# Statistics of x: from inside the pair loop to a loop of their own, in the causal-mean stage of a slot-routing block

## The chip, the cores and the metric

One Trainium2 chip, 8 cores. Each core runs the same program on its own batch element: x of 4096 x 1024 float32, all weights whole. The time is in device microseconds of the slowest core, from a run of the whole program. There is no communication between cores.

## The reference

```
# per core: x is [4096, 1024]
def ln(v): return (v - mean(v)) / sqrt(var(v) + 1e-5)       # over the 1024 columns

u   = ln(x)
m_t = mean of u[0..t]            # causal softmax of zeros: a running mean over rows
x2  = x + ln(m)
y   = ffn(ln(x2))                # routing with top 8 of 64 slots, slot update (GRU),
                                 # slot attention, layer norm, two 1024x1024 products,
                                 # and the slots spread back over the 4096 rows
out = x2 + ln(y)
```

Only the part up to x2 is touched by the change.

## The kernel before, in words

x stays in SBUF as `sb_x`, 32 tiles of 128 rows by 1024 columns, loaded by eight DMAs of four tiles each on the SP queue (`semX[0..7]`, L252). Everything up to the first matmul of the stage also waits for the weights `sb_w1b` and a short initial product.

The program is written by hand, engine by engine; each engine executes its instructions in the order in which they are written, and semaphores tie the engines together. `Guard.emit` counts VectorE's instructions in `sSVG` and ScalarE's in `sSSG`, so that a wait for `V(("cC", pr), 0)` is a wait for one named instruction.

The causal-mean stage works in pairs of tiles (`NPAIR` = 16) and groups of four tiles (`NG` = 8):

- VectorE, per group: eight half-tile `bn_stats` of x into `bn6x`, eight small instructions (`combine`) that make a mean and a variance per row (`cA`), a wait for ScalarE's square root (`sq1`), and three small instructions (`post`, `pA`) that make scale and bias.
- ScalarE, per tile: `x1b` = scale * x + bias in bfloat16 (four buffers).
- TensorE, per tile j: the triangular matrix times x1b(j), plus, for odd j, the matrix of ones times x1b(j-1), plus the carry row, into `pcs[j % 3]`; and the column totals of the pair into `ptot`. Once per pair ScalarE copies `ptot` to the one-row `carry` (`cv`), which the next pair needs.
- VectorE, per pair: four `bn_stats` of `pcs` into `bn6c`, `combine` (`cC`), a wait for `sq2`, and `post` (`pC`).
- ScalarE, per tile: `anb` = the normalised running mean, from `pcs`; POOL adds it to `sb_x` (L432).

VectorE's program today is one loop over groups: the statistics of a group of x, then two pairs of the running mean. ScalarE's loop over tiles runs, at each even tile, first `sq2` of the pair before, then the carry copy, then (at every fourth tile) `sq1` of the group, then `x1b` of this tile and `anb` of the tile two before. POOL also issues seven weight casts (float32 to bfloat16 in HBM, L290 to L296) once all loads of x have landed.

After the stage come: routing (L475 to L600), slot input, the slot update with streamed weights, and the output stage.

Of the kernel before, what the change touches and what calls it, by code (L numbers as in the profile page):

```python
# [9 lines left out]
AF = mybir.ActivationFunctionType  # L10
# [16 lines left out]
NT = 32  # L27
D = 1024
DH = 512
# [50 lines left out]
def _build(stage, prev=None):  # L80
    V = (prev or {}).get
# [35 lines left out]
    with es:  # L117
# [6 lines left out]
        c_e2 = sbt("s_e2", [P, NT])  # L124
        c_one = sbt("s_one", [P, P], BF16)
        stat = sbt("stat", [P, 16 * NT])
        SM_MX, SM_VX, SM_G1, SM_S1, SM_B1 = 0, 1, 2, 3, 4
        SM_MC, SM_VC, SM_G2, SM_S2, SM_B2 = 5, 6, 7, 8, 9
# [31 lines left out]
        sCS = sem("sCS"); sBS = sem("sBS"); sX2 = sem("sX2")  # L160
# [3 lines left out]
        sSVG = sem("sSVG"); sSSG = sem("sSSG")  # L164
# [3 lines left out]
        val = {}  # L168
# [3 lines left out]
        def VTT(out, a, b_, op):  # L172
            return gv.emit([out], [a, b_], lambda: v_.tensor_tensor(out, a, b_, op=op))  # L173

        def VTS(out, a, s1, s2, op0, op1=None):
            ins = [a] + [x for x in (s1, s2) if x is not None and not isinstance(x, float)]
            if op1 is None:
                return gv.emit([out], ins, lambda: v_.tensor_scalar(out, a, s1, None, op0=op0))  # L178
            return gv.emit([out], ins, lambda: v_.tensor_scalar(out, a, s1, s2, op0=op0, op1=op1))

        def VSTT(out, a, scl, b_, op0, op1, accum=None):
            ins = [a, b_] + ([scl] if not isinstance(scl, float) else [])
            outs = [out] + ([accum] if accum is not None else [])
            return gv.emit(outs, ins, lambda: v_.scalar_tensor_tensor(  # L184
                out, a, scl, b_, op0=op0, op1=op1, accum_out=accum))

        def VRED(out, a, op, absv=None):
            return gv.emit([out], [a], lambda: v_.tensor_reduce(
                out, a, axis=AX, op=op, apply_absolute_value=absv))

        def VBN(out, a):
            return gv.emit([out], [a], lambda: v_.bn_stats(out, a))  # L192
# [4 lines left out]
        def VRC(out, a):  # L197
            return gv.emit([out], [a], lambda: v_.reciprocal(out, a))
# [4 lines left out]
        def SACT(out, in_, func, bias=0.0, scale=1.0, accum=None):  # L203
            extra = [x for x in (bias, scale) if not isinstance(x, float)]
            outs = [out] + ([accum] if accum is not None else [])
            return gs.emit(outs, [in_] + extra,
                           lambda: s_.activation(out, in_, func, bias=bias, scale=scale,  # L207
                                                 accum_out=accum))

        def SC(k, j, n=1):  # L210
            return stat[:, k * NT + j:k * NT + j + n]

        def combine(km, kv, bn6, pj, n, extra_e2):
            view = bn6[:].rearrange("p (j g k) -> p j g k", k=3, g=4)[:, pj:pj + n]
            mus = view[:, :, :, 1]
            cvs = view[:, :, :, 2]
            t0 = tmp4[:, 0:4 * n].rearrange("p (j g) -> p j g", g=4)
            a2 = tmp4[:, 16:16 + n]
            b1_ = tmp4[:, 20:20 + n]
            b2_ = tmp4[:, 24:24 + n]  # L220
            b3_ = tmp4[:, 28:28 + n]
            c1_ = tmp4[:, 32:32 + n]
            VRED(SC(km, pj, n), mus, OP.add)
            VTT(t0, mus, mus, OP.mult)
            VRED(a2, cvs, OP.add)
            VRED(b1_, t0, OP.add)
            VTT(b2_, SC(km, pj, n), SC(km, pj, n), OP.mult)
            if extra_e2 is None:
                VTS(b3_, a2, 1.0 / 1024.0, EPS, OP.mult, OP.add)
            else:  # L230
                VSTT(b3_, a2, 1.0 / 1024.0, extra_e2, OP.mult, OP.add)
            VSTT(c1_, b1_, 0.25, b3_, OP.mult, OP.add)
            return VSTT(SC(kv, pj, n), b2_, -1.0 / 16.0, c1_, OP.mult, OP.add)

        def post(ks, kb, kg, km, pj, n, sco=40):
            VRC(SC(ks, pj, n), SC(kg, pj, n))
            VTS(tmp4[:, sco:sco + n], SC(km, pj, n), -0.25, None, OP.mult)
            return VTT(SC(kb, pj, n), tmp4[:, sco:sco + n], SC(ks, pj, n), OP.mult)

        NG = NT // 4  # L240
        NPAIR = NT // 2
# [14 lines left out]
        def _(g):  # L256
# [17 lines left out]
        bn6c = sb1("bn6c", [P, NT * 12])  # L274
        pcs = [es1.enter_context(nc.psum_tensor("pcs0", [P, D], F32)),
               es1.enter_context(nc.psum_tensor("pcs1", [P, D], F32))]
# [57 lines left out]
        @blk.vector  # L334
        def _(v):
            v.wait_ge(semC, 64)
            for g in range(NG):
                v.wait_ge(semX[g], 16)
                for j in range(4 * g, 4 * g + 4):
                    VBN(bn6x[:, j * 12:j * 12 + 6], sb_x[:, j * D:j * D + DH])  # L340
                    VBN(bn6x[:, j * 12 + 6:j * 12 + 12], sb_x[:, j * D + DH:(j + 1) * D])
                val["cA", g] = combine(SM_MX, SM_VX, bn6x, 4 * g, 4, None)
                v.wait_ge(sSSG, V(("sq1", g), 0))
                val["pA", g] = post(SM_S1, SM_B1, SM_G1, SM_MX, 4 * g, 4)
                for pr in (2 * g, 2 * g + 1):
                    if pr >= 1:
                        v.wait_ge(sSSG, V(("sq2", pr - 1), 0))
                        val["pC", pr - 1] = post(SM_S2, SM_B2, SM_G2, SM_MC, 2 * (pr - 1), 2, sco=44)
                    v.wait_ge(sCS, 2 * pr + 2)
                    for j in (2 * pr, 2 * pr + 1):  # L350
                        VBN(bn6c[:, j * 12:j * 12 + 6], pcs[j % 3][:, 0:DH])
                        val["bn6c", pr] = VBN(bn6c[:, j * 12 + 6:j * 12 + 12], pcs[j % 3][:, DH:D])
                    val["cC", pr] = combine(SM_MC, SM_VC, bn6c, 2 * pr, 2, c_e2[:, 2 * pr:2 * pr + 2])
            v.wait_ge(sSSG, V(("sq2", NPAIR - 1), 0))
            val["pC", NPAIR - 1] = post(SM_S2, SM_B2, SM_G2, SM_MC, 2 * (NPAIR - 1), 2, sco=44)

        @blk.scalar
        def _(sc):
            sc.preload_act_table(AF.Sqrt)
            sc.wait_ge(sINI, 2)  # L360
            pass
            for j in range(NT + 3):
                if j >= 2 and j % 2 == 0 and (j - 2) // 2 < NPAIR:
                    pr = (j - 2) // 2
                    sc.wait_ge(sSVG, V(("cC", pr), 0))
                    val["sq2", pr] = SACT(SC(SM_G2, 2 * pr, 2), SC(SM_VC, 2 * pr, 2), AF.Sqrt)
                if j >= 1 and j % 2 == 0 and (j // 2 - 1) < NT // 2:
                    sb_i = j // 2 - 1
                    sc.wait_ge(sBS, sb_i + 1)
                    val["cv", sb_i] = SACT(carry[:], ptot[0:1, :], AF.Identity)  # L370
                if j % 4 == 0 and j < NT:
                    g = j // 4
                    sc.wait_ge(sSVG, V(("cA", g), 0))
                    val["sq1", g] = SACT(SC(SM_G1, 4 * g, 4), SC(SM_VX, 4 * g, 4), AF.Sqrt)
                if j < NT:
                    sc.wait_ge(sSVG, V(("pA", j // 4), 0))
                    if j >= 4:
                        sc.wait_ge(sCS, j - 3)
                        sc.wait_ge(sBS, (j - 2) // 2)
                    val["x1", j] = SACT(x1b[:, (j % 4) * D:(j % 4 + 1) * D],  # L380
                                        sb_x[:, j * D:(j + 1) * D], AF.Identity,
                                        bias=SC(SM_B1, j), scale=SC(SM_S1, j))
                if j >= 2 and (j - 2) < NT:
                    jj = j - 2
                    sc.wait_ge(sSVG, V(("pC", jj // 2), 0))
                    if jj >= 3:
                        sc.wait_ge(sX2, jj - 2)
                    val["an", jj] = SACT(anb[:, (jj % 3) * D:(jj % 3 + 1) * D],
                                         pcs[jj % 3][:], AF.Identity,
                                         bias=SC(SM_B2, jj), scale=SC(SM_S2, jj))  # L390
# [839 lines left out]
```

## Time and profile before

| | us |
|---|---|
| median of 4 runs | 872.04 (870.32 to 876.44) |
| profiled execution | 872.29 |
| its span, slowest core (5) | 870.7 |
| causal-mean stage on core 5, from the first bn6x to the last bn6c | 71.75 to 313.07 |

The profile is of the slowest core. The chain of waits starts at the end and follows each step back to what released it; its rows give start, duration, engine, what is written, the line, and how many instructions are merged. `bn6x` is the statistics of x (also used again in later stages), `bn6c` those of the running mean.

### The profile page before, as it was taken

How to read it: one execution, taken by the hardware profiler on the slowest of the kernel's cores; microseconds unless marked ns; L12 is line 12 of the kernel's file. 1: busy time of each engine (PE TensorE's matmuls, PEld its weight loads, DVE VectorE, ACT ScalarE, POOL GpSimd, SP SyncE). 2: the span in 40 equal slices, each digit the busy share in tenths (PEclk: the TensorE clock that was granted, in tenths of full speed). 3: DMA queues.
4: the chain of work that ended last, by engine and by line, in shares of the span. 5: the costliest groups of instructions: out<-in, count | busy, mean ns of one | idle time of the engine just before them, and what ended most of it. 6: DMA issues, size and time to landing. Idle time of an engine off the chain costs nothing.

```text
span 870.7 us, 7011 instructions; the slowest of 8 cores (861.9 to 870.7 us)
## 1 busy us (share of the span) xinstructions
PE 358.1 (41%) x1737; PEld 129.3 (15%) x1737; DVE 342.9 (39%) x1049; ACT 275.8 (32%) x344; POOL 163.2 (19%) x91
## 2 busy tenths in 40 slices
PE   0002363454436336688683246631123565222220
PEld 0001000000000003334342222211111111000000
DVE  0004535443452556564511015550020202888883
ACT  0001343434234254655833017720001101233332
POOL 2001242233324240000000010000000000665564
PEclk9999555555555555879985555555555555555555
DMA  7996989999890001000003540025513132224224
GB/s 202 250 281 173 121 97 122 108 108 118 100 121 0 0 8 30 1 1 2 1 1 73 108 74 0 2 60 121 114 32 108 45 87 62 96 97 176 113 99 191
DMA packets 69287, 76.29 MB, mean 88 GB/s; under 512 B 53216, under 2 KB 57312, under 8 KB 68640
## 3 DMA queue, kind: packets, MB, share of 16 engines
q0 software_dynamic: 4800, 22.25, 22.6%
q1 hardware_dynamic: 64448, 53.60, 20.9%
q8 instruction: 15, 0.25, 0.1%
q14 instruction: 24, 0.20, 0.1%
HBM read 68.72 MB, written 36.70 MB: 121 GB/s over the span
## 4 chain that ended last, share of the span: by engine, by line
PE 30%; DVE 30%; DMA 13%; issue 8%; ACT 8%; another core or an unknown queue 8%; DVEq 1%; POOLq 0%; ACTq 0%; POOL 0%; SPq 0%
DVE bn6x L192 11%; PE p_h L564 8%; DVE tmp L173 6%; DVE bn6c L192 5%; DMA whhT<-wih_bf 4%; DMA whhT<-whh_bf 4%; PE pcs L406 4%; PE pcs L414 3%; ACT x1b L207 2%; PE p_si L678 2%; PE ptot L418 2%; PE pcs L410 2%; PE p_xt L594 1%; ACT x2bf L207 1%
## 5 line engine op out<-in xcount | busy, mean ns | idle before, releaser
L207 ACT ACTIVATE stat<-stat 128x2 f32<-128x2 f32 (+1 forms) x64 | 13.1, 204 | 296.9 <-DVE stat L184 295.0
L432 POOL TENSOR_TENSOR sb_x<-anb,sb_x 128x1024 f32<-128x1024 f32 x32 | 74.3, 2340 | 164.7 <-ACT anb L207 164.7
L1158 POOL TENSOR_TENSOR sb_x<-fnb,sb_x 128x1024 f32<-128x1024 f32 x32 | 74.2, 2337 | 78.1 <-ACT fnb L207 78.1
L406 PE MATMUL pcs<-x1b,s_tri 128*128 128x512 bf16 x64 | 32.8, 615 | 130.4 <-ACT x1b L207 130.4
L192 DVE BATCH_NORM_STATS2 bn6c<-pcs 128x6 f32<-128x512 f32 x64 | 39.8, 685 | 117.1 <-PE pcs L414 111.8
L192 DVE BATCH_NORM_STATS2 bn6x<-sb_x 128x6 f32<-128x512 f32 x128 | 77.5, 678 | 0.0
L564 PE MATMUL p_h<-x3t,sb_w1a 128*128 128x512 bf16 x256 | 72.2, 452 | 12.2 <-DVE bn6x L192 7.9
L1109 PE MATMUL p_f<-sb_sv,sb_alphaT 64*128 64x512 bf16 x64 | 31.8, 606 | 83.7 <-ACT fnb L207 76.1
L207 ACT ACTIVATE x2bf<-sb_x,stat 128x1024 bf16<-128x1024 f32 x32 | 36.4, 1137 | 51.6 <-PE p_at L684 51.5
L207 ACT ACTIVATE x3b<-sb_x,stat 128x1024 bf16<-128x1024 f32 x32 | 38.0, 1233 | 46.1 <-DVE stat L173 27.1
L192 DVE BATCH_NORM_STATS2 bn6x<-p_f 128x6 f32<-128x512 f32 x64 | 39.9, 685 | 18.5 <-PE p_f L1109 18.2
L195 DVE COPY x3t<-p_xt 128x1024 bf16<-128x1024 bf16 x32 | 22.1, 692 | 51.3 <-PE p_xt L594 50.5
L207 ACT ACTIVATE x1b<-sb_x,stat 128x1024 bf16<-128x1024 f32 x32 | 39.2, 1228 | 6.5 <-DVE tmp L178 5.8
L207 ACT ACTIVATE fnb<-p_f,stat 128x1024 f32<-128x1024 f32 x32 | 36.8, 1199 | 11.8 <-DVE stat L173 11.8
L678 PE MATMUL p_si<-x2bf,sb_alpha 128*64 128x512 bf16 x64 | 32.5, 612 | 19.5 <-DVE m8b L201 14.7
L207 ACT ACTIVATE anb<-pcs,stat 128x1024 f32<-128x1024 f32 x32 | 37.8, 1184 | 0.0
L173 DVE TENSOR_TENSOR tmp<-stat 128x2 f32<-128x2 f32 (+1 forms) x48 | 36.6, 763 | 0.3 <-issue 0.3
L731 POOL DMA_DIRECT2D sb_bz<-bih x1 | 0.5, 517 | 192.2 <-PE p_gh L668 192.2
L564 PEld LDWEIGHTS p_h<-x3t,sb_w1a 128*128 128x128 bf16 x256 | 28.3, 113 | 53.6 <-issue 34.4
L594 PE MATMUL p_xt<-s_eye,x3b 128*128 128x128 bf16 x256 | 20.0, 230 | 30.9 <-ACT x3b L207 30.7
L418 PE MATMUL ptot<-x1b,s_tri 128*1 128x512 bf16 x64 | 30.2, 573 | 0.0
L739 POOL DMA_DIRECT2D sb_brow<-bvp x1 | 0.5, 532 | 157.6 <-PE p_v L917 157.6
(170 smaller groups left out, 524.1 us busy)
## 6 DMA issues: line engine op xcount, KB each, us to landing
sb_x<-x SPq DMA_DIRECT2D x8, 2048.0 KB, 39.2
out<-sb_x SPq DMA_DIRECT2D x8, 2048.0 KB, 6.6
whh_bf<-Whh POOLq DMA_DIRECT2D x1, 6144.0 KB, 60.5
wih_bf<-Wih POOLq DMA_DIRECT2D x1, 6144.0 KB, 117.4
wv_bf<-wv POOLq DMA_DIRECT2D x1, 2048.0 KB, 145.5
wvp_bf<-wvp POOLq DMA_DIRECT2D x1, 2048.0 KB, 163.3
wo_bf<-wo POOLq DMA_DIRECT2D x1, 2048.0 KB, 179.0
wst<-wv_bf SPq DMA_DIRECT2D x8, 256.0 KB, 2.5
```

The costliest lines, as they stand in the source:

```text
L173: return gv.emit([out], [a, b_], lambda: v_.tensor_tensor(out, a, b_, op=op))
L192: return gv.emit([out], [a], lambda: v_.bn_stats(out, a))
L207: lambda: s_.activation(out, in_, func, bias=bias, scale=scale, accum_out=accum))
L406: ins = t.matmul(b[:, h * DH:(h + 1) * DH], c_tri[:], x1t[:, h * DH:(h + 1) * DH], start=True, stop=(j == 0))
L414: ins = t.matmul(b[:, h * DH:(h + 1) * DH], c_tri[0:1, :], carry[:, h * DH:(h + 1) * DH], start=False, stop=True)
L418: ins = t.matmul(ptot[0:1, h * DH:(h + 1) * DH], c_tri[:, 127:128], x1t[:, h * DH:(h + 1) * DH], start=(j % 2 == 0), stop=(j % 2 == 1 and ...
L432: g.tensor_tensor(sb_x[:, j * D:(j + 1) * D], anb[:, (j % 3) * D:(j % 3 + 1) * D], sb_x[:, j * D:(j + 1) * D], op=OP.add).then_inc(sX2, 1)
L564: ins = t.matmul(p_h4[jc][:, 0:DH], w1av[:, dc, jc * P:(jc + 1) * P], x3t4[:, dc * DH:(dc + 1) * DH], start=(dc == 0), stop=(dc == 7))
L594: ins = t.transpose(p_xt[j % 2][:, dc * P:(dc + 1) * P], x3v[:, dc * P:(dc + 1) * P], c_eye[:])
L678: t.matmul(p_si[0:NS, h * DH:(h + 1) * DH], alv, x2v[:, h * DH:(h + 1) * DH], start=(j == 0), stop=(j == NT - 1))
L1109: ins = t.matmul(pf[:, h * DH:(h + 1) * DH], sb_alphaT[:, j * P:(j + 1) * P], sb_sv2[:, h * DH:(h + 1) * DH], start=True, stop=True)
L1158: g.tensor_tensor(sb_x[:, j * D:(j + 1) * D], fnb[:, (j % 4) * D:(j % 4 + 1) * D], sb_x[:, j * D:(j + 1) * D], op=OP.add).then_inc(sX5, 1)
```

## The change

VectorE's loop over groups now holds only the statistics of x; the sixteen pairs follow it in a loop of their own. On ScalarE the eight square roots `sq1` stand in a loop ahead of the loop over tiles instead of inside it. TensorE, POOL and SP are not edited.

```diff
@@ VectorE
                 v.wait_ge(sSSG, V(("sq1", g), 0))
                 val["pA", g] = post(SM_S1, SM_B1, SM_G1, SM_MX, 4 * g, 4)
-                for pr in (2 * g, 2 * g + 1):
-                    if pr >= 1:
-                        v.wait_ge(sSSG, V(("sq2", pr - 1), 0))
-                        val["pC", pr - 1] = post(SM_S2, SM_B2, SM_G2, SM_MC, 2 * (pr - 1), 2, sco=44)
-                    v.wait_ge(sCS, 2 * pr + 2)
-                    for j in (2 * pr, 2 * pr + 1):
-                        VBN(bn6c[:, j * 12:j * 12 + 6], pcs[j % 3][:, 0:DH])
-                        val["bn6c", pr] = VBN(bn6c[:, j * 12 + 6:j * 12 + 12], pcs[j % 3][:, DH:D])
-                    val["cC", pr] = combine(SM_MC, SM_VC, bn6c, 2 * pr, 2, c_e2[:, 2 * pr:2 * pr + 2])
+            for pr in range(NPAIR):
+                if pr >= 1:
+                    v.wait_ge(sSSG, V(("sq2", pr - 1), 0))
+                    val["pC", pr - 1] = post(SM_S2, SM_B2, SM_G2, SM_MC, 2 * (pr - 1), 2, sco=44)
+                v.wait_ge(sCS, 2 * pr + 2)
+                for j in (2 * pr, 2 * pr + 1):
+                    VBN(bn6c[:, j * 12:j * 12 + 6], pcs[j % 3][:, 0:DH])
+                    val["bn6c", pr] = VBN(bn6c[:, j * 12 + 6:j * 12 + 12], pcs[j % 3][:, DH:D])
+                val["cC", pr] = combine(SM_MC, SM_VC, bn6c, 2 * pr, 2, c_e2[:, 2 * pr:2 * pr + 2])
@@ ScalarE
             sc.wait_ge(sINI, 2)
-            pass
+            for g in range(NG):
+                sc.wait_ge(sSVG, V(("cA", g), 0))
+                val["sq1", g] = SACT(SC(SM_G1, 4 * g, 4), SC(SM_VX, 4 * g, 4), AF.Sqrt)
             for j in range(NT + 3):
...
-                if j % 4 == 0 and j < NT:
-                    g = j // 4
-                    sc.wait_ge(sSVG, V(("cA", g), 0))
-                    val["sq1", g] = SACT(SC(SM_G1, 4 * g, 4), SC(SM_VX, 4 * g, 4), AF.Sqrt)
                 if j < NT:
                     sc.wait_ge(sSVG, V(("pA", j // 4), 0))
```

## Rows read from the trace of the kernel before

**Rows 1.** Chain of waits, core 5: start us, us, engine and what, line, count.
```profile
84.18 2.50 DVE bn6c L192 x4
96.78 2.50 DVE bn6c L192 x4
...
115.28 2.50 DVE bn6c L192 x4
...
127.70 2.50 DVE bn6c L192 x4
...
177.29 2.50 DVE bn6c L192 x4
...
313.07 2.50 DVE bn6c L192 x4
```

**Rows 2.** Head of the page: span of core 5, and of all cores.
```profile
span 870.7 us, 7011 instructions; the slowest of 8 cores (861.9 to 870.7 us)
```

**Rows 3.** Busy time by stage: us of PE, PEld, DVE, ACT, POOL; clock; DMA.
```profile
71.75:313.07 241.32, 111.18 (x247) 16.74 (x248) 106.65 (x377) 88.68 (x100) 73.22 (x37) 0.57 0.75 88
```

**Rows 4.** Waits, core 5, 78.9 to 316 us: total, times, longest.
```profile
DVE bn6c L192 <- PE pcs L414: 111.8, 15, 7.8
```

**Rows 5.** Instructions in time, core 5, PE (in brackets: idle before).
```profile
171.65 1.01 PE L406 MATMUL pcs<-x1b,s_tri 128*128 128x512 bf16 x2 [10.91 <-ACT x1b L207]
```

**Rows 6.** The same of core 2.
```profile
120.41 1.01 PE L406 MATMUL pcs<-x1b,s_tri 128*128 128x512 bf16 x2 [4.84 <-ACT x1b L207]
```

**Rows 7.** Instructions in time, core 5: a pair without x statistics.
```profile
146.54 2.49 DVE L192 BATCH_NORM_STATS2 bn6c<-pcs 128x6 f32<-128x512 f32 x4 [7.45 <-PE pcs L414]
...
150.41 0.20 ACT L207 ACTIVATE stat<-stat 128x2 f32<-128x2 f32 x1 [7.00 <-DVE stat L184]
150.55 1.01 ACT L207 ACTIVATE carry<-ptot 1x1024 bf16<-1x1024 f32 x1
...
151.47 1.22 ACT L207 ACTIVATE x1b<-sb_x,stat 128x1024 bf16<-128x1024 f32 x1
...
158.97 2.49 DVE L192 BATCH_NORM_STATS2 bn6c<-pcs 128x6 f32<-128x512 f32 x4 [7.76 <-PE pcs L414]
```

**Rows 8.** Instructions in time, core 5: the first group's statistics.
```profile
71.75 4.85 DVE L192 BATCH_NORM_STATS2 bn6x<-sb_x 128x6 f32<-128x512 f32 x8
...
78.02 0.20 ACT L207 ACTIVATE stat<-stat 128x4 f32<-128x4 f32 x1 [75.68 <-DVE stat L184]
...
78.66 0.16 DVE L173 TENSOR_TENSOR stat<-tmp,stat 128x4 f32<-128x4 f32 x1
78.92 2.37 ACT L207 ACTIVATE x1b<-sb_x,stat 128x1024 bf16<-128x1024 f32 x2 [0.70 <-DVE stat L173]
```

**Rows 9.** Instructions in time, core 5: the third group's statistics in the loop.
```profile
131.31 0.16 DVE L184 SCALAR_TENSOR_TENSOR stat<-tmp 128x2 f32<-128x2 f32 x1
131.41 4.84 DVE L192 BATCH_NORM_STATS2 bn6x<-sb_x 128x6 f32<-128x512 f32 x8
...
131.70 1.01 ACT L207 ACTIVATE carry<-ptot 1x1024 bf16<-1x1024 f32 x1
...
138.85 1.24 ACT L207 ACTIVATE x1b<-sb_x,stat 128x1024 bf16<-128x1024 f32 x1 [0.98 <-DVE tmp L178]
```

**Rows 10.** Instructions in time, core 5: the first weight cast issued.
```profile
81.37 0.57 POOL L290 DMA_DIRECT2D whh_bf<-Whh  x1 [74.13 <-DMA sb_x<-x]
```

**Rows 11.** The eight loads of x, from issue to landing.
```profile
DMA to landing us min/median/max: 14.0/39.2/57.1
```

**Rows 12.** DMA issues of the page: KB each, us to landing.
```profile
wo_bf<-wo POOLq DMA_DIRECT2D x1, 2048.0 KB, 179.0
```

**Rows 13.** Windows of core 5, PE: length, busy, clock, DMA share, GB/s.
```profile
171.50:178.30 6.80, 6.57 (x16) 0.60 0.81 92
...
354.00:366.00 12.00, 11.01 (x68) 0.86 0.01 1
```

**Rows 14.** The same of core 2.
```profile
120.41:127.50 7.09, 6.20 (x15) 0.63 0.79 88
```

## The prediction

> **What bounds the kernel now.** I began with the spans and clocks of the eight cores, then the busy time by stage, the chain of waits, the waits of the stretch that the change touches, and last the instructions of three short stretches. The changed code is the causal-mean stage, from 71.75 us, where VectorE starts the statistics of x, to the last `bn6c` group at 313.07 us [rows 1]: 241.3 us of a span of 870.7 (the cores lie between 861.9 and 870.7 [rows 2]). No engine is full there. PE is busy 111.2 us, DVE 106.7, ACT 88.7, POOL 73.2 [rows 3]. DVE waits 111.8 us in 15 waits for PE's `pcs`, 7.45 each [rows 4]; PE in turn waits for ACT's `x1b` (10.91 us before the burst at 171.65, 4.84 before one of core 2 [rows 5, 6]). So the stage is a ring: x1b on ACT, matmuls on PE, bn6c on DVE, sqrt and carry on ACT, next x1b. A pair of tiles costs one turn of that ring, and any DVE work placed inside the ring lengthens it.
>
> **The turn as it is now.** A pair without x statistics: bn6c starts at 146.54, sq2 at 150.41, the carry copy at 150.55, x1b at 151.47, and the next bn6c at 158.97 [rows 7]: 12.43 us. A pair with them: bn6c starts at 127.70 and the next at 146.54 [rows 1, 7], 18.84 us; the next such one is 158.97 to 177.29, 18.32. There are 16 bn6c groups (84.18 first, 313.07 last), 15 turns between them, 228.89 us. Eight are of the short kind: 12.60, 12.42, 12.43, 12.46, 12.43, 12.43, 12.41, 12.78, sum 99.96. The seven long ones take the other 128.93, 18.42 each. So the statistics of one group add 5.99 us to their turn.
>
> **Part 1, the hoist on VectorE.** The instructions are the same: 64 bn6x halves, 8 combines, 8 square roots, 8 posts. Only their place changes. In the stretch before the first pair, group 0 stands alone today: bn6x starts at 71.75, sqrt on ACT at 78.02, the last post instruction at 78.66, x1b at 78.92 [rows 8]. After the hoist seven more such blocks follow. The next block's bn6x can start about 0.10 us after the last post instruction starts (131.31 to 131.41 is such a step from one small DVE instruction to a bn6x that needs nothing of it [rows 9]), so a block is 78.66 + 0.10 - 71.75 = 7.01 us. DVE waits in each block for its own square root (inside the 7.01: its square root starts at 78.02, the last post instruction at 78.66), since the post of group g still stands ahead of the statistics of group g+1. Nothing hides this: PE, ACT and POOL have nothing to do until the first x1b. Added: 7 x 7.01 = 49.1 us.
>
> **Part 2, the square roots on ScalarE.** ACT now runs all eight before it looks at x1b(0). Behind these eight waits for VectorE's combines stand x1b(0) and, through it, every matmul, copy and addition of the stage; that is what holds PE and POOL for the 49.1 us. But the first x1b no longer waits for a post that follows the square root; post 0 was done 49 us ago. Today x1b starts 0.90 us after the square root (78.02 to 78.92); then it can follow it directly, by about 0.15 us, as the carry copy follows sq2 (150.41 to 150.55). Gain 0.7 us. So the first x1b moves by 48.4 us, to 127.3.
>
> **Part 3, what the loop gives back.** All 15 turns become short. That leaves 15 x 12.43 = 186.5, plus the three small slips that the short turns also have now (12.60 and 12.78 against 12.43, and one more among the seven longer ones): 187.2. It was 228.9, so 41.7 comes back. Why 5.99 and not 7.01: the block, when it stands in the loop, lies beside the carry copy. ACT's carry starts at 131.70, while DVE runs bn6x from 131.41, and x1b then starts at 138.85, only after the post [rows 9]; in a short turn x1b must itself wait for the carry, 0.92 us after it starts. The hoist loses that cover seven times: 7 x (7.01 - 5.99) = 7.1 us. This is the core of my forecast: the work moves from a place where 1.0 us of it was hidden to one where none is.
>
> **Part 4, the loads.** The last load of x lands near 81.3 us, where the weight casts on POOL, which wait for it, are issued (81.37); the eight take 14.0 to 57.1 us from issue to landing [rows 10, 11]. The hoisted block g needs load g at 71.75 + 7.01 g, the last at 120.8, 39 us after all have landed; the only block after the first that starts before 81.3 is block 1, at 78.8, and its load is the second on the same queue. So no block waits for data: 0. If block 1 did wait for the last one, 2.5 us. POOL's cast issues, from 81.37 (seven of about 0.5 us, as the first [rows 10]), now lie beside bn6x instead of beside PE; that costs between nothing and their whole 3.6 us, and I take nothing, because bn6x takes 4.84 us per eight at 131.41, while the casts' transfers run, and 4.85 at 71.75 before they start. The POOL additions never meet a hoisted bn6x. The casts are issued as before, and the last takes 179.0 us to land, about 264 [rows 12]; what waits for them comes after 313, so no later transfer is nearer or farther. SP's transposes start after the last addition and shift with it.
>
> **Part 5, TensorE's clock.** In the present stage the granted clock is mostly at its lower level, 1.2 GHz (0.57 is the mean [rows 3]). On core 5 five of the 16 bursts of matmuls rise to 2.4 GHz, late in the burst; the one from 171.65 is of that kind (mean 0.60) and comes after a break of 10.91 us [rows 5, 13]. Its turn took 18.32 us, where the turn from 96.78 to 115.28, without a rise, took 18.50 [rows 1]: 0.2 us. On core 2 a burst after a break of only 4.84 us rises too (mean 0.63) [rows 6, 14], so the length of the break does not decide. With all turns alike I take three raised bursts in the loop, 0.2 us each, so -0.6.
>
> **The sum.** 49.1 - 0.7 - 41.7 - 0.6 = +6.1 us, and +0.3 for a slip or two in the eight blocks (the third block of the profile has one of 0.28 us). +6.4. The profiled execution took 872.29 us for a span of 870.7; the median of four runs is 872.04. So 872.29 + 6.4 = 878.7, against the median 878.4; I say 878.5. Nothing behind the stage absorbs the shift: all later stages hang on its last bn6c. The cores already differ by 861.9 to 870.7 us through what the clock does in later stages, and a shift redraws that, which I count as 2 us either way.
>
> **Rivals.**
> A. *The cover was not worth what I think* (within 0.5%). If a group costs its turn 6.4 us and not 5.99 (18.84 - 12.43, the largest shown), seven give back 44.9 and the sum is 6.4 - 2.9 = +3.5, 875.8. For it: the other six long turns include raised bursts. Against: without a raised burst the turn from 96.78 to 115.28 is 18.50, which gives 6.07. Chance 0.12.
> B. *The clock* (the other side). Without long breaks PE might be granted 2.4 GHz early in each burst. The hidden-layer stage shows 0.86 over 354 to 366 us, with PE busy 11.01 of 12 [rows 13]. From the end of x1b (151.47 + 1.22) to bn6c at 158.97 PE has 6.28 us [rows 7]; wholly at 2.4 GHz that could be 3.1 us shorter, with the rise halfway 1.6. From 0.43 us per turn (6.4/15) the change breaks even. At 1.6, 15 turns give 24.0 us: 854.7. Against it: the short turns of the profile already have the spacing that the loop would have, and none of the eight is faster than 12.41. Chance 0.05, of which 0.01 is a rise from the start of every burst. The Trainium skill (TensorE: Matmul & The Clock Gate, Part 1) says that the throttled state is the default and sustained activity releases it, which would speak for B; by a released clock in every burst from the start the time would be 872.3 + 6.4 - 15 x 3.1 = 832. By the rows above, the trace agrees only in part: sustained activity raises the clock in 5 bursts of 16.
> C. *The hoisted blocks run slower* than the one of today, beside POOL's cast issues and the cast transfers: +3.6 us, 882.3. For it speaks only that no row shows a bn6x beside a cast being issued; against it, that eight of them took 4.84 us beside the casts' transfers [rows 9] and 4.85 before [rows 8]. Chance 0.08.
> D. *The slowest core is redrawn*: same mechanism, but -2 to -4 us because core 5, now the slowest, gets a better run in later stages: 875. Chance 0.10.
>
> **How the numbers follow.** My forecast has 0.65. Its own range, from blocks of 6.9 to 7.2 us (1.0 us each way over seven) and 2 us of redraw, is 875.5 to 881.5. The range that holds 8 in 10 takes in A, D and most of C: 873.5 to 882. A measurement of this kernel can tell about 0.5% from no change, 4.4 us, so slower means over 876.4 us. The forecast gives slower in 9 of 10, C always, A and D a third: 0.585 + 0.08 + 0.07 = 0.74, and slower 0.75 with rounding; faster is B and a trace of D, 0.06; within 0.5% the rest, 0.19.
>
> **What would show it.** Right: eight bn6x blocks at 71.75, 78.8, 85.8 and so on, 7.0 us apart; first x1b near 127.3; 16 bn6c groups 12.4 us apart from 132.6; the last near 319.5 instead of 313.07; no long break of PE inside the loop; DVE's waits for pcs at 15 x 7.5 us. Wrong: bn6c groups under 12 us apart with a granted clock well over 0.57 in the loop (B); blocks over 7.3 us (C); a first turn above 12.6 or turns of 13, which would mean that something besides the statistics lay in the long turns.

## The result

The changed kernel is slower, by less than forecast: 875.36 us (median of 43 runs, 872.11 to 881.88) against 873.21 us (64 runs), ratio 1.0029, 95% interval 1.0018 to 1.0040, which is +2.5 us (the difference of the two medians is 2.2). The forecast was +6.4. A second comparison, with ten runs of it (878.84) beside 24 of the kernel before (873.48), gave 1.0052 (1.0025 to 1.0079), which is +4.6 us.

The profiled execution of the changed kernel took 875.38 us, with core spans from 865.5 to 873.8 us; core 4, the least, and core 6, the largest (as long as core 2):

```profile
core 4: 865.5 us, clock 0.649
...
core 6: 873.8 us, clock 0.633
```

The slowest is now core 6. Its chain of waits, as in [rows 1], shortened to four of the eight blocks, the first turn and the last:

```profile
69.80 4.86 DVE bn6x L192 x8
76.82 4.86 DVE bn6x L192 x8
84.20 4.86 DVE bn6x L192 x8
...
119.23 4.86 DVE bn6x L192 x8
125.62 1.22 ACT x1b L207
130.85 2.50 DVE bn6c L192 x4
...
143.01 2.50 DVE bn6c L192 x4
...
304.01 2.50 DVE bn6c L192 x4
...
316.79 2.50 DVE bn6c L192 x4
```

The eight blocks stand 7.0 us apart (7.38 once, with a slip). The first x1b comes 55.8 us after the first bn6x, where it was 7.17 [rows 8]: +48.6, forecast +48.4 and a slip of 0.3. The fifteen turns take 185.94 us instead of 228.89, forecast 186.6 (187.2 less 0.6 for the clock). The stage from first bn6x to last bn6c, answering [rows 3]:

```profile
69.80:316.79 246.99, 113.90 (x247) 16.72 (x248) 106.94 (x377) 87.77 (x100) 73.19 (x37) 0.64 0.74 88
```

VectorE's busy time is what it was (106.94 against 106.65), the stage is 5.67 us longer than core 5's of before. Its waits for `pcs`, as in [rows 4], grew by 3.2 us: a wait is 7.3 to 7.8 us in every turn now, where on core 5 of before those that end a long turn were 6.9 to 7.5 us (7.45 in [rows 7]):

```profile
DVE bn6c L192 <- PE pcs L412: 115.0, 15, 7.8
```

The last square root and the first x1b show Part 2: 0.11 us between their starts, where 0.90 was [rows 8].

```profile
125.49 0.20 ACT L207 ACTIVATE stat<-stat 128x4 f32<-128x4 f32 x1 [6.80 <-DVE stat L184]
125.60 2.36 ACT L207 ACTIVATE x1b<-sb_x,stat 128x1024 bf16<-128x1024 f32 x2
```

So the stage did what was forecast and the total did not. The rest of this document is about the difference.

**How I account.** One execution gives eight cores. For each I take from its chain of waits two lengths: A, from the first bn6x to the last bn6c, and B, from the last bn6c to the first `p_gh` product, which is the hidden-layer stage. For a whole kernel I use the mean over its profiled cores. Beside it stands the mean over the eight cores' spans in all executions of a kernel, against those of the kernel before that ran on the same chip beside it. It needs no profile and is not moved by which core happens to be the slowest. A difference of two such means is good to about 1 us (95%), a difference of two means of B over 24 and 32 cores to about 1.2 us.

### The profile page after: what moved, and what is told of

Read it like the earlier page. It is cut to its first block, busy times and chain, and to the rows that moved or that the text cites. A ratio compares the mean times of both kernels' runs of the same rounds, so it can differ in the third digit from the quotient of the medians.

```text
span 873.8 us, 7011 instructions; the slowest of 8 cores (865.5 to 873.8 us)
## 1 busy us (share of the span) xinstructions
PE 358.6 (41%) x1737; PEld 128.4 (15%) x1737; DVE 343.3 (39%) x1049; ACT 274.9 (31%) x344; POOL 163.2 (19%) x91
## 4 chain that ended last, share of the span: by engine, by line
DVE 30%; PE 30%; DMA 13%; issue 9%; ACT 8%; another core or an unknown queue 8%; DVEq 1%; POOLq 0%; ACTq 0%; POOL 0%; SPq 0%
DVE bn6x L192 11%; PE p_h L562 8%; DVE tmp L173 6%; DVE bn6c L192 5%; DMA whhT<-whh_bf 4%; DMA whhT<-wih_bf 4%; PE pcs L404 4%; PE pcs L412 3%; ACT x1b L207 2%; PE p_si L676 2%; PE ptot L416 2%; PE pcs L408 2%; PE p_xt L592 1%; PE p_gh L660 1%
## 5 line engine op out<-in xcount | busy, mean ns | idle before, releaser
L562 PE MATMUL p_h<-x3t,sb_w1a 128*128 128x512 bf16 x256 | 68.3, 434 | 12.2 <-DVE bn6x L192 7.9
L562 PEld LDWEIGHTS p_h<-x3t,sb_w1a 128*128 128x128 bf16 x256 | 27.3, 109 | 50.7 <-issue 29.1
L592 PE MATMUL p_xt<-s_eye,x3b 128*128 128x128 bf16 x256 | 20.2, 230 | 30.8 <-ACT x3b L207 30.4
L416 PE MATMUL ptot<-x1b,s_tri 128*1 128x512 bf16 x64 | 31.2, 589 | 0.0
L412 PE MATMUL pcs<-carry,s_tri 1*128 1x512 bf16 x60 | 30.2, 603 | 0.0
```

Of the source, the lines that this page charges most:

```text
L412: ins = t.matmul(b[:, h * DH:(h + 1) * DH], c_tri[0:1, :], carry[:, h * DH:(h + 1) * DH], start=False, stop=True)
L416: ins = t.matmul(ptot[0:1, h * DH:(h + 1) * DH], c_tri[:, 127:128], x1t[:, h * DH:(h + 1) * DH], start=(j % 2 == 0), stop=(j % 2 == 1 and ...
L562: ins = t.matmul(p_h4[jc][:, 0:DH], w1av[:, dc, jc * P:(jc + 1) * P], x3t4[:, dc * DH:(dc + 1) * DH], start=(dc == 0), stop=(dc == 7))
L592: ins = t.transpose(p_xt[j % 2][:, dc * P:(dc + 1) * P], x3v[:, dc * P:(dc + 1) * P], c_eye[:])
```

## What the clock does in the hidden-layer stage

B in the kernel before is not one number. These are the chains of two cores of the same execution: the eight products with w1, each of 32 matmuls, then the first p_gh. Core 5, behind the bn6c at 313.07 [rows 1]:

```profile
338.87 9.66 PE p_h L564 x32
353.95 8.75 PE p_h L564 x32
369.53 9.69 PE p_h L564 x32
386.05 9.96 PE p_h L564 x32
402.84 8.41 PE p_h L564 x32
418.08 7.07 PE p_h L564 x32
431.98 8.75 PE p_h L564 x32
447.57 9.92 PE p_h L564 x32
464.77 1.45 PE p_gh L662 x24
```

Core 2:

```profile
310.67 2.50 DVE bn6c L192 x4
336.84 8.75 PE p_h L564 x31
...
366.74 6.85 PE p_h L564 x31
380.64 6.85 PE p_h L564 x31
394.54 6.85 PE p_h L564 x31
...
455.86 1.45 PE p_gh L662 x24
```

The same 32 matmuls take 7.07 us where the clock is at 2.4 GHz all through and up to 9.96 where it rises on the way. Core 5 has one group of the short kind, core 2 three in a row (its rows lack one matmul record each, hence 6.85). B is 151.70 us on core 5 and 145.19 on core 2. My reading is that B goes by the place at which a core stands against the rises of its clock when it enters the stage, and that place can be read in the loop ahead of it; the two delays further down test it. Four windows of core 5, each with one of its five rises, show the rises coming 30.7 us apart (the clock is the third number from the end: 0.55 to 0.83 where a rise falls into the window, 0.50 without one; 0.55 puts the rise 0.10 us before the window's end, at 176.90, and the others come to 207.62, 238.34 and 299.78):

```profile
176.00:177.00 1.00, 1.00 (x3) 0.55 0.00 0
207.00:208.00 1.00, 1.00 (x4) 0.69 0.87 98
238.00:239.00 1.00, 1.00 (x4) 0.83 0.00 0
...
299.00:300.00 1.00, 1.00 (x4) 0.61 0.00 0
```

One group of the kernel before lasts 18.29 + 12.43 = 30.7 us too. Not every group has a rise (core 5 shows none between 88 and 177 us), but from the second group on a rise falls into the same burst of its group: on cores 0, 1, 4, 5 and 6 the burst after the statistics of x, on cores 2, 3 and 7 the other one (core 2's is the burst of [rows 6, 14]). That is what I call the two places. B is 148.3 or 151.7 us from the first and 145.2 or 147.1 from the second.

The entry of the hidden-layer stage shows the places too. Its first product starts 25.8 us after the last bn6c on every core (26.2 where the rows lack matmul records), so up to there B is the same for all. The first rise of the clock after the last bn6c comes 31.1 us behind it on the five cores of the first place and 30.0 us on the three of the second. Core 5, where 0.93 puts the rise at 344.14, and core 2, where 0.67 puts it at 340.66 (the last bn6c stand at 313.07 and 310.67):

```profile
344.00:345.00 1.00, 1.00 (x6) 0.93 0.00 0
...
340.00:341.00 1.00, 1.00 (x5) 0.67 0.00 0
```

## The experiments

**The changed kernel again.**

> The changed kernel again, beside the kernel before, for the spans and the clock of all cores in more executions. Stage theory (the hoist costs 7 blocks of 7.01 us less 0.7, and returns 42.2 us in the loop): from the first bn6x to the last bn6c +6.5 us on every core, as in the first profile. Theory P (where a core's stage ends against the rises of its clock decides how long the hidden-layer stage takes): in the kernel before, every core leaves the causal-mean stage in one of two places and takes 148.3 to 151.7 or 145.2 to 147.1 us for the hidden-layer stage; in the changed kernel the places are scattered and the mean is about 147.2, so 1.5 to 3 us come back. Rival M (only the largest of eight cores moved by chance): the mean over cores rises by the whole 6.5 us and the hidden-layer stage is as long as before (148.9).

A is 61.03 + 185.90 = 246.9 us, as in the first profile (61.04 + 185.78). B is 147.5 on the mean, from 144.6 to 151.9 in more than two places. The mean over the cores' spans is 871.0 us in 10 runs against 866.5 in 24 of the kernel before: +4.6, not the +6.5 of rival M.

**The kernel before, three more profiles.** They were expected to show whether the two places are a habit or an accident.

> The kernel before, one more profile of eight cores. Theory P: again every core ends the causal-mean stage in one of two places, with rises 30.7 us apart; hidden-layer stage 145.2 to 147.1 us from the one, 148.3 to 151.7 from the other, mean over 148. Rival: scattered places and a mean of 147.2 as in the changed kernel, and then the 2 to 3 us lost between stage and total are not explained by it.

> The kernel before, a third profile of eight cores, to count how its cores fall on the two places: hidden-layer stage of 148.3 to 151.7 us from the one, 145.2 to 147.1 from the other, none between.

> A fourth, for the same count. Mean of the hidden-layer stage over the four profiles 148 to 148.6 us.

Over four executions B is 148.9, 147.6, 149.7 and 149.7. All 32 cores stand in one of the two places, 19 in the first and 13 in the second, and 12 take 151.7 us. The last rise in the loop starts 13.3 us before the last bn6c on the 19, and 0.7 us before it on the 13. The second profile alone, 147.6, missed its expectation of over 148: six of its cores stood in the better place. The mean of the four is 149.0, above the 148 to 148.6 expected.

**The changed kernel, a third profile.**

> The changed kernel, a third profile: stage again 247.0 us from the first bn6x to the last bn6c, hidden-layer stage 146.8 to 147.6 us on the mean, from more than two places.

A 246.9, B 147.0. Over three executions of the changed kernel B is 147.2 on the mean and only 3 of 24 cores take 151.5 us or more. The first rise after the last bn6c comes at four places now: 29.0 to 29.1 us behind it on seven of the 24 cores (B 147.5 to 147.6, once 144.6), 30.3 to 30.4 on ten (145.5), 31.0 on three (148.2, twice 151.6) and 31.2 to 31.3 on four (148.5, once 151.9). So 7 of 24 cores stand at about 31 us, where 19 of 32 stood in the kernel before. The change thus costs 246.9 - 240.5 = +6.4 us in A and gives back 149.0 - 147.2 = 1.7 us (before rounding) in B: +4.6.

**A delay behind the stage.** In the kernel before, ahead of the hidden-layer stage:

```diff
+            v.wait_ge(sX2, 4)
+            for k in range(3):                      # or range(6)
+                VBN(bn6x[:, 6 * k:6 * k + 6], sb_x[:, 0:DH])
             for g in range(NG):
                 v.wait_ge(sX2, 4 * g + 4)
```

> The kernel before, with three spare half-tile statistics (1.9 us) on VectorE behind the causal-mean stage, ahead of the hidden-layer stage. Theory P (the place of the start against the clock's rises sets the length of the hidden-layer stage): the loop still ends in its two usual places, but both are moved by 1.9 us; the cores that took 148.3 to 151.7 us take 144.6 to 147.6, the others 147 to 150 with the delay taken off; mean over cores +0 to +1 us, total between -0.5 and +1. Rival M (no such effect, only the largest of eight): +1.9 us on the mean and on the total.

> The same with six spare halves, 3.7 us. Theory P: the rises of the clock in the trace come in steps that 3.7 us nearly fills, so the start falls in nearly the old places and the delay is paid in full: hidden-layer stage without the delay 148.5 to 149.5 us on the mean, total +3.5 to +4.5. Rival M: +3.7 too. A rival that says a later start is always better for the clock: +1 or less.

Three spare instructions made the kernel faster: 867.96 us against 873.02, ratio 0.9946 (0.9925 to 0.9967). B, with the delay inside it, is 146.2 us on the five cores of the first place and 145.5 on the three of the second. Rival M falls. Theory P had the gain in the first place, but it had the second place wrong, which was to take 147 to 150 us without the delay, and the total, which was to stay within -0.5 and +1. Of the 5 us in the total 3.5 are in the mean over the cores; the rest is that the cores lie closer together, so that the slowest is nearer to the mean.

The delay is smaller than its instructions. Three spare halves take 1.8 us, but the first product starts only 0.67 us later (26.46 after the last bn6c instead of 25.79). In the kernel before, the first combine behind the stage has an instruction that takes 1.28 us and ends with the last of POOL's additions (324.00 and 323.96); with the spare halves ahead of it POOL is done, and it takes 0.17 us. Core 5, before and with three spare halves:

```profile
322.72 1.28 DVE L173 TENSOR_TENSOR tmp<-bn6x 128x16 f32<-128x16 f32 x1
...
321.09 0.17 DVE L173 TENSOR_TENSOR tmp<-bn6x 128x16 f32<-128x16 f32 x1
```

With six spare instructions the product starts 2.45 us later. B is 151.6 on six cores and 154.0 on two; total 875.24, ratio 1.0025 (1.0011 to 1.0040), mean over cores +3.5 us. The total rose by 2.2 us, less than the +3.5 to +4.5 of theory P and the +3.7 of rival M; the mean over the cores fits both, so this run does not separate them. What falls is the rival that a later start is always better. Together the two delays speak for theory P: 0.67 us later lowers B by 3.0 us on the mean, 2.45 us later raises it by 3.3. This is core 0 with three spare halves; it has three short groups in a row, where core 5 of before had one:

```profile
308.74 2.50 DVE bn6c L192 x4
...
365.54 7.07 PE p_h L567 x32
379.44 7.07 PE p_h L567 x32
393.34 7.07 PE p_h L567 x32
...
454.97 1.45 PE p_gh L665 x24
```

**The same delay ahead of the loop.**

```diff
+            v.wait_ge(semX[0], 16)
+            for k in range(3):
+                VBN(bn6x[:, 6 * (k + 9):6 * (k + 9) + 6], sb_x[:, 0:DH])
             for g in range(NG):
                 v.wait_ge(semX[g], 16)
```

> The same three spare halves (1.9 us) ahead of the first statistics instead of behind the stage. Theory P with the loop holding the cores in its two places: the delay ahead of the loop does not change where the cores end, so it is paid in full on the mean over cores, +1.5 to +2.5 us, and the two groups of hidden-layer times stay. If the loop does not hold them: the places move by 1.9 us and the total changes by 0 to 1 us, as in the kernel with the same delay behind the stage.

873.50 us, ratio 1.0005 (0.9990 to 1.0021); mean over cores +0.5 us, not +1.5 to +2.5. The loop did hold the cores in two places: B is 148.5 on six cores and 145.4 on two. But none of the six took 151.7. So my statement that it would be paid in full was wrong: the places stayed, slightly moved (the first rise 31.3 and 30.2 us behind the last bn6c instead of 31.1 and 30.0), and the costly branch of the first was gone (B 147.7 on the mean, 1.3 us less, against 1.8 us of delay).

**The delay in the changed kernel.** Same edit as behind the stage.

> The changed kernel with the three spare halves (1.8 us) behind the causal-mean stage, which made the kernel before 5 us faster. Theory P: the changed kernel's cores end the stage in scattered places already, so moving all of them by 1.8 us changes nothing on the mean; the delay is paid, mean over cores +1 to +2.5 us against the changed kernel, total 877 to 881. Rival (the spare halves themselves help, for instance by letting POOL finish its additions before VectorE's small instructions come): again several us faster than without, total 870 to 873.

877.18 us, ratio to the kernel before 1.0058 (1.0037 to 1.0079); mean over cores +4.9 us against +4.6 without the delay, each against the kernel before that ran beside it. The rival, that spare halves help by themselves, falls as the source of the gain: the 5 us are not repeated. Its mechanism is there, though, at 1.1 us, since here too the instruction beside POOL's addition takes 0.17 us instead of 1.28 and the first product starts only 0.67 us later. The total is just inside what P expected; the delay cost +0.3 us instead of +1 to +2.5 (B 147.3 with it inside), which within the noise is the 0.67 us that it really was.

**A longer group in the old order.**

```diff
+                VBN(bn6x[:, j * 12 + 6:j * 12 + 12], sb_x[:, j * D + DH:(j + 1) * D])
                 val["cA", g] = combine(SM_MX, SM_VX, bn6x, 4 * g, 4, None)
```

> The kernel before, with one half-tile statistics more per group (done twice, same result), in the old place. It lengthens each long turn by 0.7 us and leaves the order alone. Theory P: the period of a group no longer repeats the same place against the clock's rises; the eight cores leave the stage in scattered places, the hidden-layer stage averages 147 to 148 instead of 148.9, and the total rises by 2 to 4 us, not by the 5.5 us that eight spare halves cost. Rival M: total +5.5 us, the cores as before in two groups.

879.26 us, ratio 1.0073 (1.0047 to 1.0099). This one went against theory P as I had put it, and the total fits rival M better (+5.8 us by the medians, +5.5 expected). The eight halves cost 7.3 us in A, more than 5.5. On core 1 nine halves take 5.64 us where eight took 4.85, so a spare one costs 0.79 us, against 0.59 for the spare ones above (11 in 6.62 us); it repeats the write just before it, and that it waits for that write is my reading. The rest, 1.0 us, I did not trace. B fell only to 148.0, and the cores stood in three places, not in rival M's two and not scattered. Mean over cores +5.8 us.

**All posts behind all statistics.** The changed kernel with one loop more:

```diff
                 val["cA", g] = combine(SM_MX, SM_VX, bn6x, 4 * g, 4, None)
+            for g in range(NG):
                 v.wait_ge(sSSG, V(("sq1", g), 0))
-                val["pA", g] = post(SM_S1, SM_B1, SM_G1, SM_MX, 4 * g, 4)
+                val["pA", g] = post(SM_S1, SM_B1, SM_G1, SM_MX, 4 * g, 4, sco=40 + 8 * (g % 2))
```

> The changed kernel, with the posts of all eight groups behind all their statistics, so that VectorE waits for no square root between blocks. A block should be 6.1 us instead of 7.01, the first bn6c 6.3 us earlier than in the changed kernel, the loop unchanged at 185.8 us; total 868.5 to 870.5, 6 us under the changed kernel and about 4 us under the kernel before. Rival: the block stays at 7.0 because something else than the wait sets it; no difference from the changed kernel.

871.34 us, ratio 0.9985 (0.9960 to 1.0009), slightly over the range expected. The blocks are 6.1 us (core 1):

```profile
84.56 4.86 DVE bn6x L192 x8
90.66 4.86 DVE bn6x L192 x8
96.76 4.85 DVE bn6x L192 x8
```

Without VectorE's wait for its own square root a hoisted block costs 6.1 us, nearly the 5.99 that it cost in the old place, where that wait was paid but the carry copy ran beside the statistics.

**The statistics in VectorE's wait.** Group g+1 is computed while TensorE works on pair 2g+1:

```diff
+            xstat(0)
+            xpost(0)
+            for pr in range(NPAIR):
...
+                if pr % 2 == 1 and (pr + 1) // 2 < NG:
+                    xstat((pr + 1) // 2)
                 v.wait_ge(sCS, 2 * pr + 2)
...
+                if pr % 2 == 1 and (pr + 1) // 2 < NG:
+                    xpost((pr + 1) // 2)
```

with `sq1` of that group on ScalarE behind `anb` of tile 4g+1.

> Statistics of group g+1 placed in VectorE's wait for pair 2g+1 (7.45 us, against 4.85 + 1.3 us of work), its square root on ScalarE after anb of that pair, its post behind the combine of the pair. Theory C (it is the cover that decides, a block costs what of it stands outside VectorE's waits): nearly nothing remains of the seven blocks, every turn 12.4 to 12.8 us, the stage 41 us shorter than before, total 829 to 835 us. Rival (bn6x slows beside POOL's additions, or the turn is held by something else than the ring, such as PE or ACT): turns of 14 us or more, total above 850.

831.03 us, ratio 0.9525 (0.9492 to 0.9557): 41 us faster than the kernel before, and 48 us faster than the changed kernel on the same chip (878.84). Its slowest core:

```profile
107.49 2.50 DVE bn6c L192 x4
112.10 4.86 DVE bn6x L192 x8
120.10 2.50 DVE bn6c L192 x4
132.69 2.50 DVE bn6c L192 x4
137.30 4.86 DVE bn6x L192 x8
145.31 2.50 DVE bn6c L192 x4
```

A turn with statistics is 12.6 us (107.49 to 120.10, 132.69 to 145.31; the first of the seven is 13.0) and one without 12.4 to 12.6 (the last 12.8). The cover is used up: of the 8.00 us from the bn6x to the next bn6c VectorE is busy for 7.67, its wait for `pcs` is gone, and one of the small instructions takes 2.04 us where its like takes 0.15; it ends together with a POOL addition (119.54 and 119.53):

```profile
117.50 2.04 DVE L173 TENSOR_TENSOR tmp<-stat 128x4 f32<-128x4 f32 x1
```

**The account.** Changes against the kernel before (A 240.5 over 32 cores, B 149.0); the last column is the mean over the cores' spans against the runs of the kernel before on the same chip.

| kernel | A | B | A + B | spans |
|---|---|---|---|---|
| changed (24 cores) | +6.4 | -1.7 | +4.6 | +4.6 |
| posts behind | +0.8 | -2.2 | -1.3 | -1.4 |
| longer group | +7.3 | -0.9 | +6.4 | +5.8 |
| late by 3 halves | -0.1 | -3.0 | -3.1 | -3.5 |
| late by 6 halves | +0.2 | +3.3 | +3.5 | +3.5 |
| early by 3 halves | +1.6 | -1.3 | +0.3 | +0.5 |
| changed, late by 3 | +6.3 | -1.7 | +4.5 | +4.9 |
| in the wait | -40.0 | -2.1 | -42.1 | -41.8 |

The two lengths account for the spans of eight kernels within 0.6 us. (The first turn of the early one is counted from its first spare half, which puts 1.78 us more into A.)

## Why the prediction was right or wrong

- *Part 1, blocks of 7.01 us*: right, 7.00 to 7.02 with one slip. No block waited for a load.
- *Part 2, 0.7 us from the square roots*: right, 0.79.
- *Part 3, 41.7 us returned, the lost cover of 1.0 us per group*: right (42.2 on the mean of the cores). Placing the statistics where VectorE waits confirms the reason: the price of a block is the part of it that stands outside those waits.
- *Part 4, nothing for loads and casts*: right. The casts are issued from 79.58 to 83.15 us on core 6, beside the second block, whose statistics take 4.86 us; the one slip, 0.27 us, stands in its small instructions. Rival C falls.
- *Part 5, the clock in the loop*: right in size. Bursts of the loop do not rise together; rival B falls. The record of the changed kernel shows a mean clock of 0.64 over the stage on core 6 and 0.79 on core 5, which I had named as part of the sign of rival B; it is not one. Core 5, before and after 205 us:

```profile
128.57:203.00 74.43, 44.53 (x97) 6.40 (x96) 23.33 (x91) 33.52 (x36) 27.84 (x12) 1.00 0.96 107
208.00:314.00 106.00, 64.87 (x140) 9.48 (x140) 30.64 (x120) 48.81 (x52) 41.76 (x18) 0.52 0.44 49
```

  The first stretch holds six turns in 74.4 us, the second eight and a half in 106.0: 12.4 each, and 0.46 us per matmul in both, at a recorded 1.00 and at 0.52. The record reads 1.00 from the start of the execution until its first change (on the 24 cores of the changed kernel at 128 to 205 us), whatever the matmuls do.
- *"Nothing behind the stage absorbs the shift"*: this is the step that failed. The stage's +6.4 us came; the hidden-layer stage gave 1.7 us of it back, on the mean of the cores (149.0 to 147.2). That is less than half of the 3.9 us between +6.4 and the measured +2.5; the rest is under *Open*. I had taken the effect of the clock in later stages as a redraw of 2 us either way, without sign. It had a sign, because the kernel before was not a fair draw: its rises fell into the same burst of their groups, all its cores came out of the loop at one of two places, and B took 151.7 us on 12 of 32 cores, against 151.6 to 151.9 on 3 of 24 in the changed kernel. The trace of before held the warning: the lengths of B by core (three of 151.7, two of 148.3, two of 147.1, one of 145.2) and one burst per group for the rise. Where the changed kernel's cores would come out it did not show. I looked at the rises only for what they are worth inside the loop.
- *Rival A* (cover worth less) gave nearly the right time for a reason that the runs refute; *rival D* had the right place, a later stage, but put it on the slowest core alone.
- *Open*: the spans account for +4.6 us, the ratio of ten runs gives +4.6 (1.0052), but the 43 runs give +2.5. The mean over their cores is 869.7 us, 1.3 less than in the ten, and against 866.1 to 866.9 for the kernel before on three chips this is about +3.3. The remaining 0.6 or so is that their time stands 6.0 us above that mean, where it stood 6.2 to 7.0 above it in the kernel before: the slowest core was nearer to the others. I did not separate whether either is the chip, the hour, or how the cores fall on their places. Which of the two values of B a core takes from one place (148.3 or 151.7) is open too, and so is what holds the cores in two places: with a longer group they stood in three, which is no proof that the length of the group does it.

The Trainium skill (TensorE: Matmul & The Clock Gate, "HAM oscillation") warns that a kernel with idle gaps between its matmuls falls back to the throttled clock again and again. The hidden-layer stage shows it: the granted clock of core 5 rises seven times between 344 and 454 us and falls back after each, and one group of 32 matmuls takes 7.07 or 9.96 us.

## What to carry to other kernels

Ask of a moved block not how long it is but what waits beside it in the old and the new place: the same seven blocks cost 42 us in the loop, 49 ahead of it, and 2 us in a wait of 7.45 us that the profile had listed in one row. Here a loop in which the clock rose in the same burst of its rounds delivered all cores at two places, and a shift of 0.67 us ahead of a stage dense in matmuls was worth 3 us; one of 2.45 us cost more than itself. So compare the length of each later stage over all cores before believing that the rest of a kernel only shifts. And read off the trace what a delay moves: 1.8 us of instructions moved the next stage by 0.67.

## What was not expected of the hardware

An execution became 5 us faster by 1.8 us of useless work on VectorE (873.02 to 867.96), and 2 us slower by 3.6 us of it (875.24), with the same instructions everywhere else. The hidden-layer stage, with nothing changed in it or just ahead of it, took between 144.6 and 151.9 us on single cores. A VectorE instruction with two inputs of 4 or 16 columns, which takes 0.15 to 0.17 us, took 2.04 and 1.28 us beside a POOL addition and ended with it.
